# First mixer: three of the next chunk's value projections moved into the block inverse, square sums with the squares as the moving side; second mixer: its state steps as 32-wide products

## The reference

```
q, k, v = silu(conv4(x @ w_q)), silu(conv4(x @ w_k)), silu(conv4(x @ w_v));  q, k = l2norm(q), l2norm(k)
S = S * exp(g_t);  mem = k_t . S;  delta = (v_t - mem) * beta_t
S = S + outer(k_t, delta);  o_t = (q_t * scale) . S
y = rmsnorm(o) * norm_w * silu(x @ w_g) @ w_out
```

```
sa = s . a_t;  s = s * w_t + outer(sa, b_t) + outer(v_t, k_t);  y_t = s . q_t
y = groupnorm(y) * ln_w + ln_b + (r k u).v;  out = (y * gate) @ Wo.T
```

## Time and profile before

| | us |
|---|---|
| three runs | 5308.17, 5312.93, 5330.14 |
| median | 5312.93 |
| the profiled execution, its own time | 5314.12 |
| its span in the trace | 5312.3 |
| PE, DVE, ACT, POOL busy | 4563.9, 3708.1, 2767.1, 2332.2 |
| mean granted TensorE clock | 0.872 |

### The profile page before, as it was taken

The page is one execution under the profiler, slowest core; times in us unless marked ns, Lnnn a source line. Parts: engine busy times, 40 slices in busy tenths (PEclk is TensorE's granted clock), DMA queues, the critical chain, the costliest instruction groups (busy, mean ns, idle before and its releaser), DMA issues. The chain is left out here.

```text
span 5312.3 us, 119470 instructions
## 1 busy us (share of the span) xinstructions
PE 4563.9 (86%) x44570; PEld 3259.9 (61%) x44570; DVE 3708.1 (70%) x8727; ACT 2767.1 (52%) x6775; POOL 2332.2 (44%) x1892
## 2 busy tenths in 40 slices
PE   5888988999898898989799899964588788998998
PEld 3676776777676767776666466531356665655665
DVE  5666667767766777666588488556799547866874
ACT  2554545555555555544588388534200117865882
POOL 2444434444444444444476177224322126734751
PEclk7888879888887898888799899977799659998998
DMA  2000000000000000000000000000000000000000
GB/s 87 8 9 10 8 8 10 8 8 10 10 9 7 10 10 8 8 10 10 31 0 0 29 1 0 1 7 0 8 1 1 1 31 1 0 25 5 0 0 16
DMA packets 170138, 53.43 MB, mean 10 GB/s; under 512 B 142304, under 2 KB 166112, under 8 KB 168928
## 3 DMA queue, kind: packets, MB, share of 16 engines
q1 hardware_dynamic: 168160, 44.20, 3.8%
q10 hardware_dynamic: 1536, 3.21, 0.2%
HBM read 36.89 MB, written 10.49 MB: 9 GB/s over the span
## 5 line engine op out<-in xcount | busy, mean ns | idle before, releaser
L865 DVE SCALAR_TENSOR_TENSOR gd_qkT<-gd_ps,gd_w_qk,gd_qkT 128x256 f32<-128x256 f32 x768 | 367.1, 482 | 193.0 <-ACT gd_qkT L683 172.3
L430 PE MATMUL gd_ps<-gd_taps,gd_xwins 128*128 128x512 f32 x1024 | 464.8, 597 | 0.0
L1624 ACT ACTIVATE L_ffn_s<-L_ffn_s,L_ffn_nb,L_ffn_r 128x128 f32<-128x128 f32 x1024 | 419.5, 482 | 3.2
L1062 POOL TENSOR_TENSOR gd_gV<-gd_g,cst 128x512 f32<-128x512 f32 x128 | 130.4, 1042 | 621.6 <-ACT gd_X L742 621.6
L1444 POOL TENSOR_TENSOR L_ffn_t<-L_ffn_t 128x512 f32<-128x512 f32 x128 | 190.3, 1486 | 396.6 <-DVE L_ffn_t L1665 396.6
L430 PEld LDWEIGHTS gd_ps<-gd_taps,gd_xwins 128*128 128x128 f32 x1024 | 192.4, 191 | 190.9 <-issue 185.4
L1663 DVE TENSOR_TENSOR L_ffn_t<-L_ffn_ps,L_ffn_sb_rope 128x512 f32<-128x512 f32 x256 | 176.7, 690 | 101.8 <-PE L_ffn_ps L1469 101.8
L1113 POOL TENSOR_TENSOR gd_gate<-gd_gate,gd_o 128x512 f32<-128x512 f32 x128 | 159.5, 1281 | 153.3 <-DVE gd_o L959 153.3
L1512 PEld LDWEIGHTS L_ffn_ps<-L_ffn_kT,L_ffn_qT 64*64 64x64 f32 (+1 forms) x4096 | 148.5, 137 | 114.2 <-issue 98.7
L1446 POOL TENSOR_TENSOR L_ffn_r<-L_ffn_ss,L_ffn_mhalf 128x8 f32<-128x8 f32 x128 | 211.0, 1648 | 10.4 <-DVE L_ffn_ss L1687 5.2
L1453 POOL TENSOR_TENSOR L_ffn_r<-L_ffn_ss,L_ffn_mhalf 128x8 f32<-128x8 f32 x128 | 211.3, 1651 | 0.0
(11 more groups left out here) (403 smaller groups left out, 13787.9 us busy)
## 6 DMA issues: line engine op xcount, KB each, us to landing
L_ffn_sb_rope<-in_rope SPq DMA_DIRECT2D x4, 2048.0 KB, 8.4
gd_tap_row<-in_L_attn_conv_v SPq DMA_DIRECT2D x2, 2048.0 KB, 15.8
gd_blocks<-gd_nA SPq DMA_DIRECT2D x256, 16.0 KB, 1.7
gd_Z<-gd_blocks SPq DMA_DIRECT2D x32, 128.0 KB, 2.0
gd_inverses<-gd_Z SPq DMA_DIRECT2D x32, 128.0 KB, 1.7
gd_gV<-gd_inverses SPq DMA_DIRECT2D x256, 16.0 KB, 1.9
L_ffn_sb_wqkv<-in_L_ffn_wqkv SPq DMA_DIRECT2D x4, 768.0 KB, 9.3
out<-out_tok SPq DMA_DIRECT2D x8, 256.0 KB, 2.7
```

The lines of the kernel that those rows point to most:

```text
L430: ins = pe.matmul(ps[4 + i % 2][:], xwin(j)[:, t:t + P], taps[:, t, 512 * i:512 * (i + 1)], start=(t == 0), stop=(t == TAPS - 1))
L865: ins = dve.scalar_tensor_tensor(produced(j, i), ps[6 + i % 2][:, P + t:P + t + WIDE], w_tap[:, at, t:t + 1], produced(j, i), ALU.mult, AL ...
L1624: ins = act.activation(s[b][:, i, k], s[b][:, i, k], ACT.Exp, scale=r[b][:, h:h + 1], bias=nb[b][:, i, k:k + 1])
```

## The change

**Value projections.** `project_v` is replaced by `v_taps`, which issues any of the four matmuls of a quarter. Quarters 0, 1 and 2 of chunk n + 1 leave the convolution stretch and go between the stages of `solve`, into banks 0, 1 and 2; quarter 3 stays where quarter 0 was. ACT's `silu_v` of the three moves into `late`, beside the copies of the inverse. Each quarter waits for the residues of its bank (`R_s`).

**Residues.** R is now the buffer `delta` instead of `v`, so that v can be overwritten early. On DVE the four `residues` go ahead of `blocks_32`, and `decays_first` goes behind it.

**Square sums.** Eight matmuls with 32 constant columns as the stationary operand and 256 columns of squares moving, in four groups of 32 output partitions; ACT copies the sums (`copy_square_sums`), and two transposes bring them to the token's partition between the gate's second and third matmul.

**Second mixer.** DVE makes 32-wide blocks (a product of 512 instead of 2048 columns and a 32x32 transpose) for all 64 chunks before the first step; PE's transposes and ACT's copies of them are gone. Each step has eight 32x32 matmuls instead of two 128x128 ones. The output work is dealt to steps by the table `AT_Y`, ..., `AT_OUT`; `corrected` goes in halves of 8 chunks and pieces of 2, so that POOL's `S0x` products are also halved.

```diff
-        R = v
+        R = delta
...
-        SUMS = slice(448, 480)
+        SUMS = slice(WIDE, 2 * WIDE)
...
-                    for i in (2 * q, 2 * q + 1):
-                        for c in range(2):
-                            at = SUMS.start + 2 * PAIRS * c + 2 * i
-                            ins = pe.matmul(ps[6][:, at:at + 2], qk_sq[:, i, P * c:P * (c + 1)], cst[:, C_HALVES:C_HALVES + 2], start=True, stop=True)
+                    for i in range(PAIRS):
+                        if i % 2 == 0:
+                            w(sq_s.now(turn, i // 2))
+                        x, z = divmod(i, 4)
+                        ins = pe.matmul(ps[6][32 * z:32 * (z + 1), 0:WIDE], cst[:, C_HALVES + 32 * x:C_HALVES + 32 * (x + 1)], qk_sq[:, i], start=(x == 0), stop=(x == 1))
+                    ins.then_inc(ss_mm.sem, 1)
...
+                def turn_square_sums(turn):
+                    w(sbh_s.now(turn))
+                    for c in range(2):
+                        ins = pe.transpose(ps[6][:, SUMS.start + P * c:SUMS.start + P * (c + 1)], sums_by_head[:, P * c:P * (c + 1)], ident)
+                    ins.then_inc(ss_mm.sem, 1)
...
-                def solve(n):
+                def solve(n, j, follows):
...
+                    def next_v(i, *those):
+                        if follows:
+                            if those[0] == 0:
+                                w(R_s.now(n, i))
+                            v_taps(j + 1, i, i, those)
+
+                    next_v(0, 0, 1, 2, 3)
                     w(T_in.now(n))
...
+                    next_v(1, 0, 1)
...
+                    next_v(1, 2)
...
+                    next_v(1, 3)
...
+                    next_v(2, 0)
...
+                    next_v(2, 1)
...
+                    next_v(2, 2, 3)
                     for gi in range(G):
+                        if follows and gi < 3:
+                            w(v_out.now(n + 1, gi))
                         w(R_s.now(n, gi)); w(X_s.now(n, gi // 2)); w(xd_s.now(n, 3))
...
                     turn_k(n, j)
-                    for i in range(4):
-                        if follows:
-                            square_sums(n + 1, i)
-                        project_gate(n, j, i)
+                    if follows:
+                        square_sums(n + 1)
+                    project_gate(n, j, 0)
+                    project_gate(n, j, 1)
+                    if follows:
+                        turn_square_sums(n + 1)
+                    project_gate(n, j, 2)
+                    project_gate(n, j, 3)
...
-                        project_v(n + 1, j + 1, 0)
+                        v_taps(j + 1, 3, 5, range(TAPS))
...
-                        project_v(n + 1, j + 1, 1)
-                        if more:
...
+                def copy_square_sums(turn):
+                    w(ss_mm.now(turn, 0))
+                    act.activation(sums_by_head[:], ps[6][:, 0:WIDE], ACT.Copy).then_inc(sbh_s.sem, 1)
...
+                    residues(n, 0)
+                    residues(n, 1)
+                    turn_16(n)
+                    residues(n, 2)
+                    residues(n, 3)
+                    blocks_32(n)
                     if follows:
                         decays_first(n + 1)
-                    turn_16(n)
-                    residues(n, 0)
-                    residues(n, 1)
-                    blocks_32(n)
-                    residues(n, 2)
-                    residues(n, 3)
...
+SUB = 32
+AT_Y, AT_SQUARE, AT_ROOT, AT_TURN, AT_OUT = (9, 13), (22, 28), (25, 32), (28, 35), (32, 41)
...
+                    dve.tensor_tensor(Ms[b][:].rearrange("p c (h j) -> p c h j", j=RS), src, mask, ALU.mult).then_inc(m_s, 1)
+                    dve.wait_ge(m_s, n + 1)
+                    dve.transpose(MT[:, b, chunks(k)].rearrange("p c i -> p (c i)"), Ms[b][:].rearrange("p c j -> p (c j)")).then_inc(t_s, 1)
...
                     for b in range(B):
-                        ins = pe.matmul(out[:, b], MT[k % 2][:, b, j], S0[:, c, b], start=False, stop=(b == B - 1))
+                        for r in range(P // SUB):
+                            ins = pe.matmul(out[quad(r), b], MT[quad(r), b, c], S0[quad(r), c, b], start=False, stop=(b == B - 1))
...
+                for s in range(PACE):
+                    if s < CB - 1:
+                        advance(s)
+                    for b in range(B):
+                        u, piece = divmod(s - AT_Y[b], half)
+                        if 0 <= u < 2 * NBLK and piece < 4:
+                            corrected(u, b, piece)
```

More of the change, by code:

```diff
@@ L40, in constant_table @@
     t[:, C_MERGE] = i % BLOCK >= BASE
-    t[:, C_HALVES:C_HALVES + 2] = i[:, None] // HALF == np.arange(2)[None, :]
+    for x in range(2):
+        for y in range(2):
+            t[:, C_HALVES + 32 * x + 2 * x + y] = i // HALF == y
     t[:, C_EYE:C_EYE + BASE * BASE] = np.eye(BASE).reshape(1, -1)
@@ L424, in project_ab, with v_taps @@
                     pe.matmul(ps[6][:, SCORES], xwin(j)[:, PAD:PAD + P], w_ab[:], start=True, stop=True).then_inc(ab_mm.sem, 1)
[L426 to L431, removed]
+                def v_taps(j, i, at, those):
+                    for t in those:
+                        ins = pe.matmul(ps[at][:], xwin(j)[:, t:t + P], taps[:, t, 512 * i:512 * (i + 1)], start=(t == 0), stop=(t == TAPS - 1))
+                        if t == TAPS - 1:
+                            ins.then_inc(v_mm.sem, 1)
                 def project_gate(n, j, i):
@@ L659, in _ @@
                 w(conv_s.now(0))
-                for i in range(4):
-                    square_sums(0, i)
+                square_sums(0)
+                turn_square_sums(0)
                 w(ss_s.now(0))
@@ L664, in _ @@
                 for i in range(4):
-                    project_v(0, 0, i)
+                    if i >= 2:
+                        w(v_out.now(0, i - 2))
+                    v_taps(0, i, 4 + i % 2, range(TAPS))
                     produce(1, 1, i, 0, 0)
@@ L2403, in sb @@
             return ctx.enter_context(nc.sbuf_tensor("wo_" + name, shape, F32))
-        M = sb("M", [P, B, BLK, RH, RS])
+        MT = sb("MT", [P, B, CB, SUB])
+        Ms = [sb(f"Ms{b}", [P, BLK, SUB]) for b in range(B)]
         S0 = sb("S0", [P, CB, B, RS])
@@ L2427, in wkv_outputs @@
         nth = lambda k, b: B * k + b
[L2428 removed]
         by_head = lambda t: t.rearrange("p (h i) -> p h i", i=RS)
         per_head = lambda t: t.unsqueeze(2).to_broadcast([P, QUARTERS * RH, RS])
+        quad = lambda r: slice(SUB * r, SUB * (r + 1))
+        half = BLK // 2
+        PACE = (CB - 1) + 3 * BLK
         with nc.Block() as block:
@@ L2460, in gated @@
                 def gated(k, b):
-                    if not inside(k):
-                        return
                     n = nth(k, b)
@@ L2591, in _ @@
                 act.wait_ge(zero, 2)
-                for g in range(8):
-                    turned(0, g)
-                for k in range(NBLK + 2):
-                    for j in range(BLK):
-                        if BLK * k + j < CB - 1:
-                            state(BLK * k + j)
-                        if k + 1 < NBLK and j % 2 == 1:
-                            turned(k + 1, j // 2)
-                        if j in (9, 13):
-                            squares(k - 1, j // 13)
-                        if j in (10, 14):
-                            root(k - 1, j // 14)
+                act.activation(warm[:], eps[:], ACT.Sqrt, bias=eps[:], scale=1.0 / RS)
+                for s in range(PACE):
+                    if s < CB - 1:
+                        state(s)
+                    for b in range(B):
+                        k, at = divmod(s - AT_SQUARE[b], BLK)
+                        if at == 0 and 0 <= k < NBLK:
+                            squares(k, b)
+                        k, at = divmod(s - AT_ROOT[b], BLK)
+                        if at == 0 and 0 <= k < NBLK:
+                            root(k, b)
             @block.gpsimd
```

202 lines of the change are left out of this document (91 added, 111 removed).

## The result

The changed kernel takes 5276.5 us (median of 7 runs, 5261.8 to 5291.4) against 5316.9 us: ratio 0.9924, 95% interval 0.9902 to 0.9945. That is faster by 0.8%, 40 us where the forecast had 128, and 11.5 us above the range. The profiled execution took 5261.83 us.

The account below looks back on a forecast made before the run. PE was taken to bound most of the first mixer, with DVE's convolutions setting the convolution stretch's end. First mixer -53, loop openings -15, second mixer -60 gave -128 us from 5314.1: 5186, median 5185 us, range 5105 to 5265.

Parts of the forecast that it names:

- projections: First mixer: value matmuls moved into the inverse cost PE nothing there; -0.45 us a chunk in the convolution stretch.
- square sums: First-mixer gates: streaming sums take 1.1 us plus 0.3 for two transposes instead of 3.24, saving 1.9 us a chunk.
- loop openings: `turn_k` and gates of a loop's first chunk: -5 us at three of seven openings, -15 in all, bounds 0 and -30.
- New at clock 0.50: Second-mixer state steps: 1.8 us with a piece of outputs, 122 us in all against 161, at half clock.
- The rival on changes of shape: Second-mixer steps: changes of matmul shape leave only 25 us of the 60 gained; 5220 us, chance 10%.
- The rival that the strips do not overlap: First-mixer square sums: their strips do not overlap, costing 2.4 us for each chunk; 5260 us, chance 8%.
- first rival: First-mixer inverse: the clock falls all the same, +9.4 us a chunk, 300 us in all; 5485 us, chance 5%.
- Sum with full clock: Inverse of an even chunk, state products to L582's end: 23.2 us with twelve projections inside, against 24.2 before.
- The loss in L467 and L613 is confined to odd chunks: Query scores and output of odd chunks: about 4 us of them at half clock, +2.0 us, bounds 0 and 5.7.
- second rival: Emptied convolution stretch drags the clock down in even chunks' output and gates: 3 us a chunk, 96 us; 5281 us, 12%.
- Against: a 512-column matmul now stands behind each stage: Inverse: argument that the clock would hold, since a stretch full of such matmuls is at clock 1.00.
- clock near 1.00 through the inverse, no issue waits before L518: First-mixer inverse: a sign that the forecast is right; clock 0.50 in its second half would show it wrong.

Follow-up runs that it names:

- v_back: The change, but all four value quarters are projected in the convolution stretch again, where they stood before: 5153.8 us, ratio 0.9709.
- second_only: The kernel before the change with only the change's second-mixer outputs (`wkv_outputs`): 5235.6 us, ratio 0.9860.
- one_moved: The change with one value matmul of each inverse moved forward, so two stand ahead of below_32 (4, 2, 2, 1, 1, 1, then 1 behind): 5207.9 us, ratio 0.9791.
- even_deal: The change with its twelve value matmuls dealt two ahead of each of the six inverse stages: 5207.0 us, ratio 0.9800.
- v3_late: The change with the last value quarter put back behind the seventh produce, ahead of the next chunk's query products: 5237.9 us, ratio 0.9864.
- filler_back: The change with one additional unread 128x512 matmul in each inverse, behind merged_128: 5294.5 us, ratio 0.9948.
- two_quarters: The change with only value quarters 0 and 1 in the inverse (2, 2, 1, 1, 1, 1 ahead of its stages), the others where they stood before: 5144.7 us, ratio 0.9637.
- two_q_front: two_quarters with its eight matmuls dealt 2, 2, 2, 1, 1, 0 ahead of the six stages: 5078.6 us, ratio 0.9542.

## Why the prediction was wrong

The sum had four parts against before: projections -8 us (for 15.5 pairs: -1.45 in even chunks, +0.95 in odd ones), square sums -45, loop openings -15, second mixer -60. The projections are where it failed.

- **Second mixer: right, and low by its clock.** By medians it gave -79. In v_back, at clock 0.50, the outputs took 147.7 us, where 145 were said and 205.8 measured before: the first step came 3.7 us after the start (4.3 said), the steps took 118 us from there (122 said; one with a piece 1.89, 1.8 said), and the end 25.5 us (18 to 20 said). In the kernel after the clock was 0.50 until 4242 us and 1.00 from there to the last step; a step with a piece then took 1.18 us, and the outputs 118 us. That it stays at 0.50 was a step of the working ("New at clock 0.50") with no bound for the other level. The rival on changes of shape is out: it left 25 us of gain, and 58 were there at clock 0.50. One step at clock 0.50, with three such changes, has no idle time before any of PE's matmul records. The step in PE's order of time, and the busy time of the two halves of the steps, both of the kernel after:

```profile
4232.36 0.61 PE L2543 MATMUL wo_ps_s<-wkv_S,cst 128*128 128x16 f32 x2
4232.90 0.40 PE L2552 MATMUL wo_ps_s<-wo_S,wo_MT 32*32 32x8 f32 x16
4233.23 0.67 PE L2565 MATMUL wo_ps_y<-cst,wkv_xp 128*32 128x128 f32 x4
4233.68 0.65 PE L2566 MATMUL wo_ps_y<-wo_S0x,x0T 128*32 128x128 f32 x4
4234.26 0.61 PE L2543 MATMUL wo_ps_s<-wkv_S,cst 128*128 128x16 f32 x2
```
```profile
4197.70:4242.20 44.50, 44.50 (x647) 34.65 (x642) 14.78 (x17) 6.24 (x30) 12.33 (x6) 0.50 0.01 2
4242.30:4285.20 42.90, 42.90 (x862) 33.98 (x858) 27.86 (x32) 9.14 (x40) 17.42 (x8) 1.00 0.01 3
```

- **Square sums and loop openings: right in kind, low.** -60 said, -82 measured (v_back against second_only). The streaming sums took 1.00 us (1.1 said). In chunks whose gates DVE does not hold up, the way from `turn_k` to the state products went from 10.6 to 8.5 us (-2.1, 1.9 said); at the three cold openings it became 10 to 11 us shorter, 8 to 9 of them beyond the sums' own (5 said). The rival that the strips do not overlap is out.
- **Value projections: wrong, and this is the error.** -8 said, +123 measured by medians, +112 by the end of the first mixer (v_back against the change). By stretches, with 15.5 pairs of chunks (forecast: -1.0 and -0.6 us in the inverse, -0.45 twice, +2.0 in odd chunks; measured: the stretches of the change less those of v_back, in us):

  | | forecast | measured |
  |---|---|---|
  | inverse and delta | -25 | +103 |
  | convolution stretch | -14 | -33 |
  | output | +31 | +44 |

  So the step that failed is the inverse. It failed in two ways, and a third step was wrong in its place more than in its size.
  - *The clock holds.* In 7 of 31 chunks it did not, and each of those cost 10 us, 68 in all. This is the first rival. Its price was right (+9.4 a chunk) and it had 5%; it struck 7 chunks, half of the 14 from which it was said to decide. one_moved and even_deal, which put two matmuls at that place, took 69 us less.
  - *"Sum with full clock: 0.2 + 10.5 + 1.3 + 4.2 + 3.3 + 3.7 = 23.2 us, against 24.2"*. A good inverse took 24.8 us (952.9 to 977.7), by the starts of its groups 0.4 + 11.7 + 5.2 + 4.0 + 3.6. The small stages were sized right (5.5 said for 5.2). The twelve projections were not: one that stands alone between two stages takes 1.06 us, not 0.88. Nor were the 64-wide stages, since 3.3 us was half of what they took at clock 0.50. So even a good inverse is longer than the cold one was (24.1 to 24.2 us), by 1.1 us a chunk or 34 in all against v_back.
  - *The loss in L467 and L613 is confined to odd chunks.* The output ran at clock 1.00 in even chunks in v_back and at 0.78 with the change, and took 1.7 us more there; in odd chunks it took 1.1 us more, where 2.0 was said. Together that is 13 us beyond the forecast. It is the output half of the second rival, given 12%; the gates did not slow down.
  - The convolution stretch was no part of the error: it gave 1.1 us a chunk where 0.45 was said.
- *"Against: a 512-column matmul now stands behind each stage"* was the reason for holding the first rival at 5%. One such matmul ahead of below_32 was too little in seven chunks, and with two no fall came in the 5 us behind L533's first record; that had no row in the trace of before to be read from, and the chance should have said so.
- The mark "clock near 1.00 through the inverse, no issue waits before L518" came true in 24 chunks, any one of which would have passed for a confirmation; the count over all chunks is what tells.

## What to carry to other kernels

Work moved to keep PE's clock up must be dealt where PE's work is thinnest, and be checked over all repetitions, since a place that is just short fails in some and passes in others. Taking work out of a stretch that another engine bounds gains little and can cost the clock of what follows. When moved work turns out to be a burden, move only as much as the clock needs: against the kernel that moves none, twelve projections cost 123 us as the change deals them, between nothing and 17 us dealt well, and eight gained 75 (medians).

## What was not expected of the hardware

- The place of a matmul counted more than its work: with one unread 128x512 matmul more in each inverse, at one place or another, the kernel took 5251 and 5294 us, against 5277 without it.
- The same instructions of `wkv_outputs` took 118, 129 or 148 us in the profiled executions of thirteen kernels, with mean clocks of 0.73, 0.63 and 0.50 over the state steps. Comparisons of under one per cent between kernels here need several runs for that reason alone.
- Short idle times went with the loss of the clock: 1.19 to 1.51 us inside one small stage in the seven inverses that lost it. In the four kernels with one matmul ahead of it (after, v3_late, filler_back, two_quarters), 25 inverses had 1.08 us or more of it and all 25 were long; all that were not long had 0.98 us or less, and so had ten long ones, most of which lost the clock later. With two matmuls ahead of it no inverse of any kernel had more than 0.70 us. That the idle time makes the clock fall is not shown apart from the matmul that shortens it.
- Open: what makes that idle time long in one chunk and short in the next, with the same instructions. The long chunks are not spread evenly: six of the seven long inverses of the kernel after lie in its first ten chunks, and the 24th chunk was long in after, v3_late, one_moved, two_quarters and two_q_front. Each kernel has one profile, so whether other executions lose it in the same chunks wasn't seen. Nor was it tried whether fewer than eight projections would do.
